# Cross-attention and feed-forward layer on one core: GpSimd's 1024-column subtractions issued as four of 256 columns, its 768-column operations as three

## The chip, the cores and the metric

The kernel runs on one core of a Trainium2 chip. The metric is the device time of one execution in microseconds (us), lower is better. The engines of the core are TensorE (PE in the rows), VectorE (DVE), ScalarE (ACT), GpSimd (POOL) and SyncE (SP), which only issues transfers here. Each engine takes its instructions in the order in which the program gives them and waits at semaphores.

## The reference, cut to what matters

The input is x (2 x 512 rows of 1024 columns, float32), positions and a context of 1024 rows. One layer is computed:

```python
x = x + xattn(layernorm(x), ...)      # 256 channels of 4; 16 heads of 16
x = x + ffn(layernorm(x), ...)

# in xattn, twice (after attention, after the product with the context):
return (hs * A_full + out * B_full).reshape(b, l, H * C)      # rat_write, the residual write

# in ffn, for each of w1, w2, w3 (3584 x 1024 and its transpose):
d = w - base
coeff = mean(abs(d))
W = base + coeff * sign(d)
```

Everything is float32. In the residual write three of the four channels of a row (768 columns) are multiplied by A and have a term q subtracted or added; the fourth (256 columns) only gets a term added. `coeff` needs the mean over a whole weight, so each weight is read twice: once to measure it, once to use it.

## The kernel before

**Two phases.** Phase one (0 to about 450 us of the span) does the whole of the attention layer and, beside it, measures w1 and w3: 56 tiles of 128x1024, each loaded with its base, subtracted, and summed in absolute value on ScalarE. Every third tile is subtracted by GpSimd (`MEASURER = ("DVE", "DVE", "POOL")`), the others by VectorE. Phase two (about 450 us to the end) is the feed-forward layer. Up to about 1000 us it makes the weights w1 and w3 tile by tile and multiplies with them (lines L1501 on TensorE, written as sums and differences of blocks, seven products p1 to p7 for each pair of tiles, in three passes each); after that it multiplies with w2 (L1542) and GpSimd has nothing to do.

**Order.** The order of phase one comes from a list scheduler in the kernel file, `phase_one_order()`. Its table of times holds one of 2.35 us for a subtraction on GpSimd, and it keeps apart in time what it takes for a stretch in which VectorE and GpSimd can't both work (`shared`, `begin`). Phase two's order comes from a second planner, `ffn_order()`. Both give each engine a fixed list; the kernel walks the lists.

**GpSimd's work.** Beside powers of one to three columns (L2459) and the DMAs of w2 (L2520) it has:

- `measure(t)` (L2463): the subtraction of a tile that is measured, 18 times in phase one;
- `difference(n)` (L2468): the subtraction of weight tile n before ScalarE takes its sign, 56 times, 4 of them in phase one. ScalarE's `sign` (L1805; in phase one L1800) waits for it, VectorE's `whole_weight` (L2179) waits for the sign and makes base + coeff * sign; from that come the sums of tiles (L2191 to L2199) and the low parts for the three passes (`lower`, L2183), whose high parts ScalarE writes (L1814, L1822, L1949, L1954);
- part 9 of `rat_out`: the three channels of a residual write, `hid - q` (L2445) for the first write, `q + x` (L2450) for the second, 768 columns, 8 times each;
- part 10 of `rat_out` (L2455): the fourth channel, 256 columns, and L2505 the same columns plus x.

Part 11 on VectorE (L2157, L2160) ends a residual write. In phase two the four row buffers of w1 and w3 are loaded by SyncE (L1179, L1180) as soon as VectorE's last readers of a buffer are done:

```python
if f == 0:
    sp.wait_ge(d_lo, j - 1)
    sp.wait_ge(e_lo, j - 1)
    sp.wait_ge(f_sum, 4 * (j - 1))
```

`d_lo`, `e_lo`, `f_lo`, `g_lo` count the low parts (L2183) of the tiles. ScalarE also copies each product's bank out of PSUM before TensorE may write it again (`snap`: L1959, L1964, L1968); L1968 is the copy after p5, and p3 writes the same bank. VectorE's L2377 to L2390 are the sums of the hidden rows, half tiles of 512 columns from SBUF. TensorE in phase one also has products with a constant (L1344, `pair<-unit`) that no result needs; their number is fixed.

Of the kernel before, what the change touches and what calls it, by code (L numbers as in the profile page):

```python
# [11 lines left out]
ALU = mybir.AluOpType  # L12
# [4 lines left out]
BATCH, SEQ, HID = 2, 512, 1024  # L17
H, C, RH = 256, 4, 16
# [46 lines left out]

UNITS = 3 * JT
PARTS = 3
NB = HID // P
VW = HD + 1
VT = NH * VW + 32 - VW  # L70
# [139 lines left out]
def before(stage, t, part):  # L210
# [105 lines left out]
    elif stage == "measure":  # L316
        if part == 0:
            after("measure", t - PARTS, 2)
            if t >= LATER:
# [490 lines left out]
def bass_layer(nc: bass.Bass, d: dict, out: bass.AP):  # L810
    with ExitStack() as whole:
# [38 lines left out]
        wqkv = sba("wqkv", [P, HH, 3 * H])  # L850
        diag = [sba("diag0", [P, NB, WAYS[0], 32])]
        yn = sba("yn", [P, 3, H])
# [6 lines left out]

        xT = sba("xT", [P, NB, P])  # L860

# [26 lines left out]
        qk_xa = sba("qk_xa", [P, HID])  # L888
# [57 lines left out]
        def measured(t):  # L946

            if t % PARTS == 0:
                return part[:, 0, :], part[:, 1, :]
            n = t % PARTS - 1  # L950
            if t < LATER:
# [6 lines left out]
        ld_x = [sem(f"ld_x{t}") for t in range(TILES)]  # L958
        ld_part = [sem(f"ld_part{n}") for n in range(PARTS)]
        ld_raw = [sem(f"ld_raw{n}") for n in range(ROWS)]  # L960
# [19 lines left out]
        bk_v, fi_v, fi_q, fi_x, fi_var, fi_pow, fi_ok = sems("bk_v fi_v fi_q fi_x fi_var fi_pow fi_ok")  # L980
        me_dve, me_pool, me_abs, c_ones, c_sum, c_mm, c_ok = sems("me_dve me_pool me_abs c_ones c_sum c_mm c_ok")
        n_wk, n_t, n_hi, n_lo, eye_ok = sems("n_wk n_t n_hi n_lo eye_ok")
        f_diff, f_sign, f_w, f_sum = sems("f_diff f_sign f_w f_sum")
# [191 lines left out]
        def _(sp):  # L1175
# [23 lines left out]
            for engine, stage, t, part in order:  # L1199
                if engine != "SP":  # L1200
                    continue
                if stage == "measure":
                    n, j = divmod(t, JT)
                    if t >= PARTS:
                        sp.wait_ge(me_abs, t - PARTS + 1)
                    if t == LATER:
# [125 lines left out]
        def _(pe):  # L1332
# [5 lines left out]
            def turn_hid(t, target):  # L1338

                return turn_blocks(lambda k: hid[:, t, k * P:(k + 1) * P], NB, target)  # L1340

# [1096 lines left out]
        def _(pool):  # L2438
            def rat_out(n, stage, t, part):
                q, skip = (wr[set_of[stage, t]][k] for k in ("q", "s"))  # L2440
                ha, last = by_channel(t)[:, 0:3, :, :], by_channel(t)[:, 3, :, :]
                if part == 9:
                    pool.wait_ge(ro_q[n], t + 1)
                    if n == 0:
                        pool.tensor_tensor(ha, ha, q[:, :].rearrange("p (c k j) -> p c k j", c=C - 1, j=32), ALU.subtract  # L2445
                                           ).then_inc(bk_v, 1)
                    else:
                        pool.wait_ge(fi_v, t + 1)
                        pool.wait_ge(ld_again, again_turn(t))
                        pool.tensor_tensor(q[:, :], q[:, :], qk_xa[:, 0:3 * H], ALU.add).then_inc(fi_q, 1)  # L2450
                elif part == 10:
                    pool.wait_ge(ro_s[n], t + 1)
                    if n == 1:
                        pool.wait_ge(fi_x, t + 1)
                    pool.tensor_tensor(last, last, skip[:, :].rearrange("p (k j) -> p k j", j=32), ALU.add).then_inc(ro_skip[n], 1)  # L2455

            def factors(r, done):

                pool.tensor_tensor(r, r, power[:, 0:r.shape[1]], ALU.pow).then_inc(done, 1)  # L2459

            def measure(t):
                w, base = measured(t)
                pool.tensor_tensor(w, w, base, ALU.subtract).then_inc(me_pool, 1)  # L2463

            def difference(n):
                w, base = raws[n % ROWS]
                pool.wait_ge(ld_raw[n % ROWS], 32 * (n // ROWS + 1))
                pool.tensor_tensor(w[:, :], w[:, :], base[:, :], ALU.subtract).then_inc(f_diff, 1)  # L2468

            pool.memset(power[:, :], -0.5).then_inc(consts, 1)  # L2470
            pool.wait_ge(consts, 1)
# [125 lines left out]
```

## Time and profile before

| | |
|---|---|
| time, three runs | 1272.66 us median (1272.12 to 1275.04) |
| the profiled execution | 1270.68 us, span 1268.9 us, granted TensorE clock 0.989 |
| TensorE busy | 1185.2 us, 93% of the span |
| VectorE busy | 981.4 us, 77% |
| ScalarE busy | 694.1 us, 55% |
| GpSimd busy | 283.4 us, 22%, in 187 instructions |

A row of a timeline has start, duration and then engine, line, operation, tiles and shape; in brackets stands how long the engine had been idle and what ended that. "x2" is two instructions merged, with their common duration. An instruction that has started but can't get on shows it as a longer duration.

### The profile page before, as it was taken

How to read it: one execution, taken by the hardware profiler on the slowest of the kernel's cores; microseconds unless marked ns; L12 is line 12 of the kernel's file. 1: busy time of each engine (PE TensorE's matmuls, PEld its weight loads, DVE VectorE, ACT ScalarE, POOL GpSimd, SP SyncE). 2: the span in 40 equal slices, each digit the busy share in tenths (PEclk: the TensorE clock that was granted, in tenths of full speed). 3: DMA queues.
4: the chain of work that ended last, by engine and by line, in shares of the span. 5: the costliest groups of instructions: out<-in, count | busy, mean ns of one | idle time of the engine just before them, and what ended most of it. 6: DMA issues, size and time to landing. Idle time of an engine off the chain costs nothing. (4 is left out here: it accounts for less than half of the span.)

```text
span 1268.9 us, 17072 instructions
## 1 busy us (share of the span) xinstructions
PE 1185.2 (93%) x6298; PEld 921.5 (73%) x6298; DVE 981.4 (77%) x1287; ACT 694.1 (55%) x999; POOL 283.4 (22%) x187
## 2 busy tenths in 40 slices
PE   5889878898899599999999999999999999999998
PEld 3755455565666478888878888887788888888887
DVE  6878678867787957988887778797786777888864
ACT  4768566574455547565566655565564334334342
POOL 2223223323331212334133333232340000000000
PEclk9999999999999699999999999999999999999999
DMA  9266667865011145768667778766795877853232
GB/s 358 91 243 248 253 242 264 309 245 188 13 67 67 50 149 143 227 220 277 215 216 224 230 240 265 208 203 192 234 287 165 316 279 255 283 198 122 95 126 107
DMA packets 99062, 257.35 MB, mean 203 GB/s; under 512 B 9362, under 2 KB 23972, under 8 KB 98468
## 3 DMA queue, kind: packets, MB, share of 16 engines
q1 hardware_dynamic: 94948, 241.59, 52.7%
q0 software_dynamic: 4032, 14.68, 6.4%
q8 instruction: 50, 0.82, 0.3%
q14 instruction: 32, 0.26, 0.1%
HBM read 214.81 MB, written 41.42 MB: 202 GB/s over the span
## 5 line engine op out<-in xcount | busy, mean ns | idle before, releaser
L2004 ACT ACTIVATE split<-grid 128x1024 fp32r<-128x1024 f32 x98 | 104.0, 1061 | 160.8 <-PE pair L1542 147.4
L2468 POOL TENSOR_TENSOR raw_w<-raw_w,raw_base 128x1024 f32<-128x1024 f32 x56 | 143.5, 2579 | 214.7 <-DMA raw_base<-in_mean_w 214.2
L2412 DVE TENSOR_TENSOR split<-grid,split 128x1024 fp32r<-128x1024 f32 x98 | 119.6, 1224 | 61.9 <-ACT split L2004 61.7
L1542 PE MATMUL quad<-split 128*128 128x512 f32 x588 | 149.3, 389 | 0.5 <-DVE hid L2419 0.5
L1542 PE MATMUL pair<-split 128*128 128x512 f32 x588 | 149.2, 389 | 0.0
L1542 PEld LDWEIGHTS quad<-split 128*128 128x128 f32 x588 | 110.3, 188 | 23.7 <-DVE split L2412 0.9
L1542 PEld LDWEIGHTS pair<-split 128*128 128x128 f32 x588 | 110.4, 188 | 22.9
L1501 PE MATMUL pair<-xnT_hi,ring_hi 128*128 128x512 f32 x224 | 88.1, 393 | 9.6 <-DVE t_b_lo L2215 9.6
L1501 PE MATMUL pair<-t_b_hi,ring_hi 128*128 128x512 f32 x224 | 88.9, 397 | 4.4 <-ACT snap L1968 4.1
L2183 DVE TENSOR_TENSOR ring_lo<-raw_base,ring_hi 128x1024 fp32r<-128x1024 f32 x56 | 68.3, 1220 | 26.4 <-ACT ring_hi L1949 21.0
L1501 PE MATMUL pair<-xnT_hi,ring_lo 128*128 128x512 f32 x224 | 87.9, 392 | 0.0
L1501 PE MATMUL pair<-t_b_lo,ring_hi 128*128 128x512 f32 x224 | 87.9, 392 | 0.0
L1501 PE MATMUL pair<-xnT_lo,ring_hi 128*128 128x512 f32 x224 | 87.8, 392 | 0.0
L1501 PE MATMUL pair<-t_b_hi,ring_lo 128*128 128x512 f32 x224 | 87.2, 389 | 0.0
L2179 DVE SCALAR_TENSOR_TENSOR raw_w<-quad,coeff,raw_base 128x1024 f32<-128x1024 f32 x52 | 66.5, 1278 | 15.1 <-ACT quad L1805 14.8
L2183 DVE TENSOR_TENSOR ring_lo<-raw_w,ring_hi 128x1024 fp32r<-128x1024 f32 x28 | 40.6, 1454 | 41.1 <-ACT ring_hi L1814 41.1
L1805 ACT ACTIVATE quad<-raw_w 128x1024 f32<-128x1024 f32 x52 | 53.0, 1019 | 20.4 <-POOL raw_w L2468 20.1
L2520 POOL DMA_DIRECT2D late<-in_w x28 | 25.0, 892 | 150.9 <-ACT late L1980 150.9
L1501 PEld LDWEIGHTS pair<-xnT_hi,ring_hi 128*128 128x128 f32 x224 | 42.6, 190 | 18.8 <-issue 9.8
L2091 DVE TENSOR_REDUCE negwide<-quad 128x4 f32<-128x512 f32 (+3 forms) x32 | 46.9, 1486 | 11.9 <-PE quad L1438 11.9
L1501 PEld LDWEIGHTS pair<-t_b_hi,ring_hi 128*128 128x128 f32 x224 | 42.1, 188 | 15.4 <-ACT snap L1968 7.0
L2463 POOL TENSOR_TENSOR ctxw<-ctxw 128x1024 f32<-128x1024 f32 x14 | 34.0, 2428 | 80.2 <-DMA ctxw<-in_mean_w 80.2
(332 smaller groups left out, 2784.8 us busy)
## 6 DMA issues: line engine op xcount, KB each, us to landing
raw_w<-in_w SPq DMA_DIRECT2D x56, 512.0 KB, 5.4
raw_base<-in_mean_w SPq DMA_DIRECT2D x56, 512.0 KB, 6.7
grid<-h_blocks SPq DMA_DIRECT2D x49, 512.0 KB, 3.7
ctxw<-in_w SPq DMA_DIRECT2D x28, 512.0 KB, 4.0
ctxw<-in_mean_w SPq DMA_DIRECT2D x28, 512.0 KB, 5.2
late<-in_mean_w SPq DMA_DIRECT2D x28, 512.0 KB, 7.5
late<-in_w POOLq DMA_DIRECT2D x28, 512.0 KB, 6.2
grid<-in_mean_w SPq DMA_DIRECT2D x28, 512.0 KB, 4.7
```

The costliest lines, as they stand in the source:

```text
L1501: a = pe.matmul(bank, ww[:, at + k, :], xx, start=first and k == 0 and n == 0, stop=k == half - 1 and n == 2, skip_group_check=not first)
L1542: a = pe.matmul(into[t], found[:, a, t * P:(t + 1) * P], found[:, b, :], start=p == 0 and n == 0 and q < 4, stop=p == PAIRS - 1 and n == 2 ...
L1805: act.activation(spare.rearrange("p a b -> p (a b)"), w[:, :], ACT.Sign).then_inc(f_sign, 1)
L2004: act.activation(splits[n % RINGS][:, 0:2, :], operands(n), ACT.Copy).then_inc(a_hi, 1)
L2091: a = dve.tensor_reduce(found.rearrange("p r j -> p (r j)"), quad[:, :, at:at + cols], AX.X, ALU.max, negate=True)
L2179: dve.scalar_tensor_tensor(w[:, :], sign, coeff[:, k:k + 1], base[:, :], ALU.mult, ALU.add).then_inc(f_w, 1)
L2183: dve.tensor_tensor(whole_of(pair[1]), source, whole_of(pair[0]).bitcast(F32), ALU.subtract).then_inc(done, 1)
L2412: dve.tensor_tensor(found[:, 2:4, :], operands(n), found[:, 0:2, :].bitcast(F32), ALU.subtract).then_inc(a_lo, 1)
L2463: pool.tensor_tensor(w, w, base, ALU.subtract).then_inc(me_pool, 1)
L2468: pool.tensor_tensor(w[:, :], w[:, :], base[:, :], ALU.subtract).then_inc(f_diff, 1)
L2520: pool.dma_start(lates[n % LATES][:, :], d["w2"][n], accum_op=ALU.add).then_inc(ld_add[n % LATES], 16)
```

## The change

GpSimd's `measure` and `difference` issue four subtractions of 256 columns in place of one of 1024. The two forms of part 9 issue three operations of 256 columns, one for each channel, in place of one of 768. Only the last instruction of a group adds to the semaphore. The planners' tables and all other engines' lists stay as they are.

```diff
+QUARTERS = 4
...
                     if n == 0:
-                        pool.tensor_tensor(ha, ha, q[:, :].rearrange("p (c k j) -> p c k j", c=C - 1, j=32), ALU.subtract
-                                           ).then_inc(bk_v, 1)
+                        for c in range(C - 1):
+                            a = pool.tensor_tensor(ha[:, c], ha[:, c], q[:, c * H:(c + 1) * H].rearrange("p (k j) -> p k j", j=32),
+                                                   ALU.subtract)
+                        a.then_inc(bk_v, 1)
                     else:
                         pool.wait_ge(fi_v, t + 1)
                         pool.wait_ge(ld_again, again_turn(t))
-                        pool.tensor_tensor(q[:, :], q[:, :], qk_xa[:, 0:3 * H], ALU.add).then_inc(fi_q, 1)
+                        for c in range(C - 1):
+                            some = slice(c * H, (c + 1) * H)
+                            a = pool.tensor_tensor(q[:, some], q[:, some], qk_xa[:, some], ALU.add)
+                        a.then_inc(fi_q, 1)
...
+            def subtract(w, base):
+
+                for n in range(QUARTERS):
+                    some = slice(n * HID // QUARTERS, (n + 1) * HID // QUARTERS)
+                    a = pool.tensor_tensor(w[:, some], w[:, some], base[:, some], ALU.subtract)
+                return a
+
             def measure(t):
                 w, base = measured(t)
-                pool.tensor_tensor(w, w, base, ALU.subtract).then_inc(me_pool, 1)
+                subtract(w, base).then_inc(me_pool, 1)
 
             def difference(n):
                 w, base = raws[n % ROWS]
                 pool.wait_ge(ld_raw[n % ROWS], 32 * (n // ROWS + 1))
-                pool.tensor_tensor(w[:, :], w[:, :], base[:, :], ALU.subtract).then_inc(f_diff, 1)
+                subtract(w, base).then_inc(f_diff, 1)
```

GpSimd's list at about 310 to 332 us, before the change: the residual writes of two tiles (`hid` and `wr_q` are the rows and q) and the first four differences (`raw_w`).

```order
66 L2445 TENSOR_TENSOR hid<-hid,wr_q 128x3x8x32
67 L2455 TENSOR_TENSOR hid<-hid,wr_s 128x8x32
68 L2468 TENSOR_TENSOR raw_w<-raw_w,raw_base 128x1024 x2
69 L2459 TENSOR_TENSOR stat_back<-stat_back,power 128x2
70 L2468 TENSOR_TENSOR raw_w<-raw_w,raw_base 128x1024
```

The same place after the change (the line numbers have moved):

```order
66 L2447 TENSOR_TENSOR hid<-hid,wr_q 128x8x32 x3
67 L2461 TENSOR_TENSOR hid<-hid,wr_s 128x8x32
68 L2471 TENSOR_TENSOR raw_w<-raw_w,raw_base 128x256 x8
69 L2465 TENSOR_TENSOR stat_back<-stat_back,power 128x2
70 L2471 TENSOR_TENSOR raw_w<-raw_w,raw_base 128x256 x4
```

Nothing has changed places; the tile of 768 columns is three instructions, each tile of 1024 is four.

GpSimd's list at the end of phase one and the start of phase two (from about 415 us) before the change, with the last two second residual writes, L2450 and L2455:

```order
91 L2450 TENSOR_TENSOR wr_q<-wr_q,qk_xa 128x768
92 L2455 TENSOR_TENSOR hid<-hid,wr_s 128x8x32
93 L2505 TENSOR_TENSOR hid<-hid,qk_xa 128x8x32
94 L2450 TENSOR_TENSOR wr_q<-wr_q,qk_xa 128x768
95 L2455 TENSOR_TENSOR hid<-hid,wr_s 128x8x32
96 L2459 TENSOR_TENSOR x_stat<-x_stat,power 128x1 x2
97 L2468 TENSOR_TENSOR raw_w<-raw_w,raw_base 128x1024
98 L2520 DMA late<-in_w 128x1024
99 L2468 TENSOR_TENSOR raw_w<-raw_w,raw_base 128x1024 x3
```

And after it:

```order
91 L2455 TENSOR_TENSOR wr_q<-wr_q,qk_xa 128x256 x3
92 L2461 TENSOR_TENSOR hid<-hid,wr_s 128x8x32
93 L2518 TENSOR_TENSOR hid<-hid,qk_xa 128x8x32
94 L2455 TENSOR_TENSOR wr_q<-wr_q,qk_xa 128x256 x3
95 L2461 TENSOR_TENSOR hid<-hid,wr_s 128x8x32
96 L2465 TENSOR_TENSOR x_stat<-x_stat,power 128x1 x2
97 L2471 TENSOR_TENSOR raw_w<-raw_w,raw_base 128x256 x4
98 L2533 DMA late<-in_w 128x1024
99 L2471 TENSOR_TENSOR raw_w<-raw_w,raw_base 128x256 x12
```

Again nothing has moved past anything else; between the pieces of one tile stands no other instruction of GpSimd. The lists of TensorE, VectorE, ScalarE and SyncE are the same but for line numbers.

## Rows read from the trace of the kernel before

**Rows 1.** Windows: us, busy time (instructions) per engine, PEclk, DMA share, GB/s

```profile
core 0: us, PE busy (x) PEld busy (x) DVE busy (x) ACT busy (x) POOL busy (x), PEclk, DMA share, GB/s
0.00:450.00 450.00, 374.51 (x2738) 256.98 (x2739) 350.18 (x627) 269.24 (x478) 125.09 (x107) 0.97 0.50 186
450.00:1000.00 550.00, 545.62 (x2395) 445.65 (x2394) 431.54 (x478) 321.51 (x421) 158.32 (x80) 1.00 0.69 221
```

**Rows 2.** Waits of TensorE: who, for whom, us in total, times, longest

```profile
PE pair L1501 <- DVE t_b_lo L2215: 9.6, 1, 9.6
...
PE pair L1501 <- ACT snap L1968: 4.1, 3, 2.1
```

**Rows 3.** Timeline of GpSimd, operations back to back

```profile
196.95 0.72 POOL L2459 TENSOR_TENSOR stat_back<-stat_back,power 128x2 f32<-128x2 f32 x1
197.63 0.73 POOL L2505 TENSOR_TENSOR hid<-hid,qk_xa 128x256 f32<-128x256 f32 x1
...
322.28 4.68 POOL L2468 TENSOR_TENSOR raw_w<-raw_w,raw_base 128x1024 f32<-128x1024 f32 x2
```

**Rows 4.** Timeline, 709 to 716 us, GpSimd and VectorE

```profile
709.27 6.07 POOL L2468 TENSOR_TENSOR raw_w<-raw_w,raw_base 128x1024 f32<-128x1024 f32 x2
...
710.77 2.30 DVE L2183 TENSOR_TENSOR ring_lo<-raw_w,ring_hi 128x1024 fp32r<-128x1024 f32 x1 [2.10 <-ACT ring_hi L1814]
```

**Rows 5.** Groups of VectorE, 450 to 985 us: busy us, mean ns | idle before

```profile
L2191 DVE TENSOR_TENSOR raw_base<-raw_w 128x512 f32<-128x512 f32 x27 | 30.0, 1110 | 0.0
...
L2381 DVE TENSOR_TENSOR work<-work 128x512 f32<-128x512 f32 x13 | 24.1, 1850 | 1.3
...
L2347 DVE TENSOR_TENSOR work<-quad,snap 128x512 f32<-128x512 f32 x26 | 17.8, 684 | 5.8 <-ACT snap L1968 5.8
```

**Rows 6.** Timeline, collisions in phase one, VectorE and TensorE

```profile
44.80 2.29 DVE L2032 SCALAR_TENSOR_TENSOR stat_front<-stat_front 128x3 f32<-128x3 f32 x1 [0.97 <-POOL stat_front L2459]
...
324.87 2.90 DVE L2157 TENSOR_TENSOR hid<-hid,wr_a 128x768 f32<-128x768 f32 x1
...
328.82 1.09 PE L1335 MATMUL pair<-ident,hid 128*128 128x128 f32 x8 [1.13 <-DVE hid L2160]
...
332.00 2.30 DVE L2032 SCALAR_TENSOR_TENSOR stat_back<-stat_back 128x2 f32<-128x2 f32 x1 [0.82 <-POOL stat_back L2459]
...
337.55 0.27 PE L1486 MATMUL pair<-ident,wr_b 128*8 128x128 f32 x1 [1.71 <-DVE wr_b L2131]
...
378.78 1.70 DVE L2028 SCALAR_TENSOR_TENSOR x_stat<-x_stat 128x1 f32<-128x1 f32 x1
...
380.73 0.27 PE L1486 MATMUL pair<-ident,wr_b 128*8 128x128 f32 x1 [1.02 <-DVE wr_b L2131]
```

**Rows 7.** Timeline, the end of phase one, 425 to 439 us

```profile
425.91 1.83 POOL L2450 TENSOR_TENSOR wr_q<-wr_q,qk_xa 128x768 f32<-128x768 f32 x1 [4.33 <-issue]
427.70 1.70 POOL L2455 TENSOR_TENSOR hid<-hid,wr_s 128x256 f32<-128x256 f32 x1
...
426.03 4.46 DVE L2183 TENSOR_TENSOR ring_lo<-raw_w,ring_hi 128x1024 fp32r<-128x1024 f32 x2
...
431.60 0.94 DVE L2157 TENSOR_TENSOR hid<-hid,wr_a 128x768 f32<-128x768 f32 x1
...
438.45 0.76 PE L1501 MATMUL pair<-xnT_hi,ring_hi 128*128 128x512 f32 x1 [9.58 <-DVE t_b_lo L2215]
```

**Rows 8.** Timeline, one round of phase two, 850 to 871 us

```profile
850.91 2.39 POOL L2468 TENSOR_TENSOR raw_w<-raw_w,raw_base 128x1024 f32<-128x1024 f32 x1 [9.67 <-DMA raw_base<-in_mean_w]
850.92 2.93 DVE L2385 TENSOR_TENSOR s_rows<-s_rows,work 128x512 f32<-128x512 f32 x1
...
855.15 1.21 DVE L2183 TENSOR_TENSOR ring_lo<-raw_base,ring_hi 128x1024 fp32r<-128x1024 f32 x1
...
856.39 0.33 SPq L1179 DMA_DIRECT2D raw_w<-in_w  x1
...
866.10 2.39 POOL L2468 TENSOR_TENSOR raw_w<-raw_w,raw_base 128x1024 f32<-128x1024 f32 x1 [9.53 <-DMA raw_base<-in_mean_w]
...
870.16 0.50 PE L1501 MATMUL pair<-t_b_hi,ring_hi 128*128 128x512 f32 x1 [2.06 <-ACT snap L1968]
```

## Prediction

> **What bounds the kernel now.** I began with the busy times by window. From 450 to 1000 us TensorE is busy 545.6 of 550 us at full clock; before 450 us it is busy 374.5 of 450 [rows 1]. So phase two can give back about 4 us up to the point where GpSimd stops, and phase one is where time lies. Its chain passes again and again through VectorE, ScalarE and short products. The waits of TensorE then say what ends last: 9.6 us at the end of phase one on VectorE's L2215, and in phase two three waits, 4.1 us together, on ScalarE's copy L1968 [rows 2]. GpSimd is busy about a quarter of the time in both stretches, so its own length is not the question; what it does to VectorE is. One view shows that: in phase two a half-tile operation of VectorE takes 0.68 us when one input is in PSUM (L2347) but 1.11 us on average in L2191 and 1.85 us in L2381, whose inputs are both in SBUF [rows 5].
>
> **What the two do to each other.** At 710.77 VectorE starts a low part while GpSimd is in a difference that began at 709.27. It takes 2.30 us and not the 1.21 us of a free one [rows 4, 8]: it gets on at about 711.85. The second difference had been queued; the two together end at 715.34. 715.34 less 2.34 is 713.0, and VectorE's operation ends at 713.07: GpSimd, too, waited for VectorE. So one of them works at a time, for a whole instruction, and who has waited comes next, even between two queued instructions of GpSimd. The end of phase one shows it in a row of four: L2450 until 427.7, a low part, L2455 (1.70 us instead of 0.72), the second low part, 4.46 us for a pair that needs 2.35 [rows 7]. The Trainium skill, "SBUF — State Buffer", section "Who interferes with whom", states the same as a rule: a VectorE instruction with two SBUF inputs and a GpSimd instruction that reads SBUF exclude each other, and the later one blocks fully until the other ends. The trace agrees to 0.1 us. By that rule pieces cut both ways: each piece of GpSimd may have to wait for an instruction of VectorE.
>
> **The price of a piece.** GpSimd operations of 256 columns follow each other at 0.68 us (196.95 to 197.63), two of 1024 take 4.68 us, 2.34 each; the one of 768 columns gives way to the next after 1.79 us [rows 3, 7]. (2.34 - 0.68) / 768 is 2.16 ns a column, which leaves 0.13 us fixed for an instruction. Alone, a difference becomes 4 x 0.68 = 2.72 us, 0.38 us more; a residual write 2.04, 0.27 us more. The Trainium skill, "GPSIMD Engine Reference", section 3.1, gives 4497 ns for 2048 columns and about 2.6 cycles a column at 1.2 GHz, 2.17 ns; as an estimate that leaves 0.06 us fixed and 0.18 us more for a difference. The slope agrees with the rows; the fixed part doesn't, and mine stands.
>
> **Phase one.** For each collision I let pieces of 0.68 us and VectorE's next operations take turns, and cap the gain by the idle time of TensorE behind it.
> - 44.80: the three-column L2032 sits behind a whole subtraction, 2.29 us instead of 0.15. Behind a piece it loses 0.6. ScalarE's next step starts 1.6 us earlier; I count 1.0.
> - 324.87 and 332.00: L2157 takes 2.90 instead of 0.95, L2032 2.30 instead of 0.15, and TensorE idles 1.13 and 1.71 us behind them [rows 6]. A third one, at 314.45, is of the same kind on the same chain. By turns they gain 1.3 (314.45), 0.9 (324.87) and, since L2032, L2157 and L2160 then each meet a piece, only 0.2 (332.00): 2.4 in sum.
> - 378.78: the one-column L2028 takes 1.70; with a piece 0.6. TensorE idles 1.02 behind it [rows 6]: 1.0. Two like it, at 230.81 and 388.87, I put at 0.7 and 0.55.
> - The end. From 425.91: piece to 426.59, low part to 427.73, piece to 428.41, low part to 429.55, piece to 430.23, L2179 to 431.43, L2455 to 432.1, L2157 then. It starts at 431.60 now [rows 7]. VectorE there has only operations from SBUF, so each piece takes a turn: four turns of 0.68 in place of 2.1 us. Loss 0.45, and nothing hides it, for this is the wait of 9.58 us.
>
> 1.0 + 2.4 + 1.0 + 1.25 - 0.45 = 5.2 us. Not all arrives: between these places other chains of phase one are nearly as long, and the constant products of TensorE keep their number. From both sides: nothing passes but the loss (+0.45), or all (-5.2). I take 0.6 of it, nearer to all since the caps are already idle time that TensorE shows: **-3.1 us**.
>
> **Phase two.** Take the round at 850 us [rows 8]. Now the difference lies over L2385 (2.93 us), VectorE goes on, its low part ends at 856.36, SyncE issues the next load at 856.39, that lands, the next difference starts at 866.10, and TensorE has idled 2.06 us at 870.16, as the copy L1968 stands behind the sign of that difference in ScalarE's list. By turns: piece to 851.59, L2385 to 852.2, piece to 852.9, L2390 to 853.5, piece to 854.2 beside L2341 (PSUM, no collision), low part to 855.3. The load is issued 1.0 us earlier. The difference at 866.10 has VectorE idle beside it and takes 0.38 longer. The wait of 2.06 becomes about 1.4. The three waits of 4.1 us follow this pattern: 3 x 0.6 = 1.9 us. Against it: the first difference itself ends at 856.0 instead of 853.3, so ScalarE's sign, everything behind it, and VectorE's L2179 (which wants that sign) come 0.9 to 2.7 us later, and the third load of the round about 1.3 us later. What is late then are copies that TensorE wants two products later (2.7 us each), but I know no row that prices the third load. Bounds: -1.9 with no price for it, and +1.1 (3 x 0.38) with the loads no earlier, up to +4 if each of the three waits also gets that 1.3. I take **-1.0 us**. After 1000 us GpSimd does nothing and nothing changes.
>
> **Sum.** -3.1 - 1.0 = -4.1 us. The profiled execution took 1270.7 us (span 1268.9 and 1.8 around it), so its counterpart would be 1266.6. It lies 2.0 below the median of the runs, 1272.66; against that I get **1268.6 us**. A measurement of this kernel tells about 0.2% from no change, 2.5 us.
>
> **Rivals.**
> - *The gain stays local.* VectorE gets its turns sooner, but other chains of phase one end the stages, and phase two breaks even. For it: VectorE's total loss changes little where it has only SBUF work, four turns of 0.68 against one of 2.34. Against: the idle times right behind the collisions. Gain 0 to 2.5, time about 1271.5. Chance 0.26.
> - *Slower: long differences hold ScalarE's list.* In about nine of the 14 rounds the difference at the place of 850.91 grows from 2.4 to over 5 us. If the later sign delays the round's loads, the waits on L1968 grow by 0.38 + 1.3 each instead of shrinking, and rounds that now have no wait get one of about 1 us. It decides when more than three rounds do so, as then phase two costs over 5 us: about 1276. For it: such ScalarE lateness goes to a wait beyond one product, 2.7 us. Against: the first load goes out earlier. Chance 0.12.
> - *GpSimd keeps its turn between pieces.* Pieces overlap a little (0.72 us long, 0.68 apart [rows 3]); if VectorE can't get in between, a tile blocks it for 2.72 us. Each of some nine collisions on the chain costs 0.27 to 0.38 more: +3 us, 1275.5. Against: [rows 4, 7], where it got in between two queued ones. Chance 0.05.
> - *More than I count*: all of phase one's 5.2 and all of 4.1, or a chain freed that I don't see: below 1264. Chance 0.04.
>
> The forecast has 0.53, its own range is 1265 to 1270. The forecast's range reaches from its lower edge over the first rival to the border of the slower ones: 1264.6 to 1273.5. Faster by over 0.2% (below 1270.1): forecast, the last rival and a little of the first, 0.58. Slower (above 1275.2): most of the second and third, 0.15. The rest 0.27.
>
> **What the profile of the changed kernel would show.** Pieces 0.68 us apart where VectorE is idle. VectorE's L2032 at about 45 and 330 us at no more than 0.8 us; L2381 and L2191 at means near 1.0; GpSimd's busy time up by 20 us or more, most of it from waiting. A difference over the half-tile sums of over 4 us. The waits of TensorE on L1968 under 3 us in sum. The 9.58 us before L1501 about unchanged, its start some 3 us earlier. The prediction is wrong if TensorE's start there has not moved (the gain was local), or if the L1968 waits have grown or come in more than three rounds (the long differences).

## Result and the profile after

The changed kernel takes 1259.13 us (median of four, 1257.10 to 1264.21) against 1273.85 of before in the same comparison: ratio 0.9888, 95% interval [0.9853, 0.9923], 14.3 us less (9.8 to 18.7). A second comparison of the same kernel, the run `again` below, gave 1260.38 and 0.9894 [0.9871, 0.9918], 13.5 us. Two executions of later comparisons, one of before with 2399 us and one of eighths_drained with 4158 us, are left out of all ratios. I had forecast 1268.6 within 1264.6 to 1273.5: the direction was right, the gain three and a half times too small, and the time is outside the range.

The page after, first the busy times, then the chain of work that ended last:

```profile
PE 1188.3 (94%) x6298; PEld 925.6 (74%) x6298; DVE 952.1 (76%) x1287; ACT 696.0 (55%) x999; POOL 355.1 (28%) x441
...
PE 86%; DVE 7%; ACT 5%; issue 2%; POOL 0%; DMA 0%; SPq 0%; DVEq 0%; ACTq 0%
```

GpSimd is 71.7 us busier, VectorE 29.3 us less. The windows of after, to be set beside [rows 1]:

```profile
0.00:450.00 450.00, 383.77 (x2762) 265.04 (x2763) 341.20 (x630) 273.14 (x482) 146.25 (x205) 0.95 0.51 186
450.00:1000.00 550.00, 549.58 (x2415) 449.97 (x2414) 418.36 (x482) 324.12 (x422) 208.82 (x236) 1.00 0.72 228
```

TensorE is busy 9.3 us longer in the first 450 us, at a mean granted clock of 0.95 instead of 0.97, and has 24 more products behind it. In the 550 us after that it stands still for 0.4 us where it stood 4.4. Its waits, first of before (those that [rows 2] doesn't have), then of after:

```profile
PE pair L1418 <- DVE negwide L2091: 7.1, 11, 1.6
...
PE quad L1445 <- DVE negwide L2091: 4.0, 3, 2.7
PE pair L1486 <- DVE wr_b L2131: 3.9, 5, 1.7
```

```profile
PE pair L1502 <- DVE t_b_lo L2216: 9.2, 1, 9.2
...
PE pair L1419 <- DVE negwide L2092: 4.2, 9, 0.8
...
PE quad L1446 <- DVE negwide L2092: 3.3, 2, 3.0
...
PE pair L1487 <- DVE wr_b L2132: 1.3, 3, 0.5
...
PE pair L1502 <- ACT snap L1969: 0.4, 1, 0.4
```

VectorE's groups in phase two, 450 to 985 us, beside [rows 5]: the sums from SBUF fall to means of 0.74 and 0.89 us, the form with an input in PSUM is unchanged.

```profile
L2192 DVE TENSOR_TENSOR raw_base<-raw_w 128x512 f32<-128x512 f32 x27 | 20.0, 740 | 0.0
...
L2348 DVE TENSOR_TENSOR work<-quad,snap 128x512 f32<-128x512 f32 x28 | 19.2, 685 | 9.4 <-ACT snap L1969 9.2
...
L2382 DVE TENSOR_TENSOR work<-work 128x512 f32<-128x512 f32 x13 | 11.5, 887 | 1.3
```

**Where the time went, place by place.** TensorE has the same 6298 products in the same order in both traces, so the delay of a product, its start in after less its start in before, says what has been won so far. These are the products of after that answer to 337.55, 380.73 and 438.45 us [rows 6, 7], and one ahead of them that is at 286.52 in before:

```profile
286.91 0.24 PE L1609 MATMUL pair<-csum,ones 128*128 128x2 f32 x1 [0.42 <-issue]
...
334.39 0.27 PE L1487 MATMUL pair<-ident,wr_b 128*8 128x128 f32 x1
...
376.02 0.27 PE L1487 MATMUL pair<-ident,wr_b 128*8 128x128 f32 x1
...
433.10 0.76 PE L1502 MATMUL pair<-xnT_hi,ring_hi 128*128 128x512 f32 x1 [9.25 <-DVE t_b_lo L2216]
```

The delay is +0.39, then -3.16, -4.71 and -5.35 us: 3.55 us between 287 and 335, 1.55 up to 376, 0.64 up to the end of phase one. The two waits for `wr_b` are gone. No fall of the granted clock lies between 287 and 406 us in either trace, so the first two steps are not the clock's. The rest, to -10.1 us at the end, comes at three products of phase two that waited for L1968 in before: 638, 870 and 910 us.

Before 287 us this pair of traces shows no gain on balance, and that is most likely chance. TensorE is 2.3 us ahead at 53 us; then the granted clock takes it back. It falls from 2.4 to 1.2 GHz at other places in each trace: the mean over the first 290 us is 0.99 in before and 0.96 in after. The deepest fall of after, 0.55 in 220 to 230 us, is not the work of the pieces: hold_adds below, which has none, shows 0.51 there. Nor is the one in 50 to 60 us (0.83): first_four, whole up to 314 us, shows 0.73.

The three profiled kernels that leave phase one as it was (before, p2_pieces, hold_adds below) begin phase two at 438.45, 444.12 and 444.43 us; the four with all its pieces (after, again, p1_pieces, p1_and_hold) at 433.10, 431.35, 435.01 and 433.78. The means are 9.0 us apart. The profiled run of before, at a mean clock of 0.989, was among the luckiest: 22 later runs had 0.981 to 0.989 and a median of 1275.1 us, 4.5 above it.

### The profile page after: what moved, and what is told of

Same layout as the page of the kernel before. It is cut to its first block, busy times and chain, and to the rows that moved or that the text cites. A ratio compares the mean times of both kernels' runs of the same rounds, so it can differ in the third digit from the quotient of the medians.

```text
span 1258.8 us, 17326 instructions
## 1 busy us (share of the span) xinstructions
PE 1188.3 (94%) x6298; PEld 925.6 (74%) x6298; DVE 952.1 (76%) x1287; ACT 696.0 (55%) x999; POOL 355.1 (28%) x441
## 4 chain that ended last, share of the span: by engine, by line
PE 86%; DVE 7%; ACT 5%; issue 2%; POOL 0%; DMA 0%; SPq 0%; DVEq 0%; ACTq 0%
PE pair L1502 30%; PE quad L1502 12%; PE quad L1543 10%; PE pair L1543 10%; PE pair L1483 3%; PE quad L1446 2%; PE pair L1599 2%; PE quad L1436 2%; DVE negwide L2092 2%; PE quad L1483 1%; PE quad L1599 1%; ACT prob L1747 1%; PE pair L1409 1%; PE pair L1336 1%; PE pair L1389 1%
## 5 line engine op out<-in xcount | busy, mean ns | idle before, releaser
L2471 POOL TENSOR_TENSOR raw_w<-raw_w,raw_base 128x256 f32<-128x256 f32 x224 | 199.3, 950 | 184.7 <-DMA raw_base<-in_mean_w 184.7
L2184 DVE TENSOR_TENSOR ring_lo<-raw_base,ring_hi 128x1024 fp32r<-128x1024 f32 x56 | 71.4, 1275 | 32.5 <-ACT ring_hi L1950 25.7
L2471 POOL TENSOR_TENSOR ctxw<-ctxw 128x256 f32<-128x256 f32 x56 | 42.5, 790 | 75.4 <-DMA ctxw<-in_mean_w 75.4
L2092 DVE TENSOR_REDUCE negwide<-quad 128x4 f32<-128x512 f32 (+3 forms) x32 | 46.9, 1487 | 13.5 <-PE quad L1439 13.5
L1747 ACT ACTIVATE prob<-quad 128x1536 f32<-128x1536 f32 (+1 forms) x24 | 38.2, 1592 | 23.6 <-PE quad L1451 13.6
```

The lines of the kernel that those rows point to most:

```text
L1747: act.activation(probs[TURN[u] % 2][:, :, 0:cols], quad[:, :, 0:cols], ACT.Exp).then_inc(at_p, 1)
L2092: a = dve.tensor_reduce(found.rearrange("p r j -> p (r j)"), quad[:, :, at:at + cols], AX.X, ALU.max, negate=True)
L2184: dve.tensor_tensor(whole_of(pair[1]), source, whole_of(pair[0]).bitcast(F32), ALU.subtract).then_inc(done, 1)
L2471: a = pool.tensor_tensor(w[:, some], w[:, some], base[:, some], ALU.subtract)
```

## The experiments

Each is timed against before in one of four comparisons, in which before had medians of 1273.5 to 1275.9 us; so the ratios can be set side by side, the medians only roughly. "Idle" is what TensorE stood still between 15 us and its first product of phase two, without the last wait, the one of 9.1 to 10.3 us right ahead of that product. "p5 waits" are those on the copy L1968 (L1969 or L1970 in the changed kernels). Idle, start and p5 waits come from one trace of each kernel.

| kernel | median, us | ratio, 95% interval | idle, us | phase two begins | p5 waits, us |
|---|---|---|---|---|---|
| before (profiled run) | | | 52.0 | 438.5 | 4.1 |
| again (= changed) | 1260.38 | 0.9894 [0.9871, 0.9918] | 44.3 | 431.4 | none |
| p1_pieces | 1263.25 | 0.9910 [0.9890, 0.9931] | 45.8 | 435.0 | 1.9 |
| p2_pieces | 1272.02 | 0.9985 [0.9966, 1.0004] | 54.5 | 444.1 | 0.4 |
| hold_adds | 1271.19 | 0.9977 [0.9957, 0.9997] | 51.7 | 444.4 | none |
| p1_and_hold | 1261.55 | 0.9877 [0.9859, 0.9895] | 42.5 | 433.8 | 0.3 |
| first_four | 1269.61 | 0.9954 [0.9934, 0.9974] | 51.6 | 443.5 | 3.1 |
| measure_only | 1272.66 | 0.9974 [0.9955, 0.9993] | 49.3 | 442.9 | 1.9 |
| writes_only | 1269.47 | 0.9947 [0.9925, 0.9969] | 47.7 | 437.9 | 2.5 |
| halves | 1263.88 | 0.9898 [0.9880, 0.9916] | 45.3 | 438.1 | 1.0 |
| eighths | 1273.10 | 0.9984 [0.9960, 1.0008] | 46.9 | 434.9 | 7.7 |
| eighths_drained | 1267.82 | 0.9942 [0.9920, 0.9964] | 46.3 | 439.7 | 3.3 |
| eighths_add_moved | 1273.98 | 0.9996 [0.9975, 1.0016] | 48.0 | 434.7 | 2.0 |
| quarters_drained | 1260.47 | 0.9890 [0.9860, 0.9919] | 43.6 | 435.5 | none |

**One phase at a time.** In p1_pieces and p2_pieces `subtract` gets the number of pieces:

```diff
-                subtract(w, base).then_inc(f_diff, 1)
+                subtract(w, base, QUARTERS if n < ROWS else 1).then_inc(f_diff, 1)   # p1_pieces
+                subtract(w, base, 1 if n < ROWS else QUARTERS).then_inc(f_diff, 1)   # p2_pieces, measure and part 9 whole
```

Expected of p1_pieces:

> Pieces in phase one alone (measure, both forms of part 9, the four differences of phase one); the 52 differences of phase two are whole again. If the gain of the two phases adds up, as the delay between the two traces says (5.3 us at the first product of phase two, 4.7 us more until 913 us), TensorE's first product of phase two starts near 433 us, the three waits on the copy behind p5 are back at about 4.1 us, and the time is 8 to 10 us below before (5.3 and what the profiled run of the changed kernel lost to a low granted clock before 250 us). If the gain of phase one needs the pieces of phase two, or is given back there, it is under 4 us.

Expected of p2_pieces:

> Pieces in the 52 differences of phase two alone; all of phase one as before. If the gains add up: the first product of phase two starts near 438.4 us as before, the waits on the copy behind p5 are under 0.6 us in sum, and the time is 4.7 us below before, 4 to 5.5. My recorded step (each wait shrinks by 0.6, less the price of long differences) gives 1 us.

Measured: 11.5 us (8.8 to 14.0) for phase one alone, above the 8 to 10 expected, though the interval reaches into it; 1.9 us (-0.5 to 4.3) for phase two alone, where 4 to 5.5 was expected, and by its interval not clear of zero. They add up to the 13.5 of the whole. Phase one is over four fifths of the gain. The waits on the copy are back in p1_pieces at 1.9 us, not 4.1. In p2_pieces the delay against before falls from +5.7 to +0.9 us during phase two, so 4.8 us against that trace; but p1_pieces, with phase two whole, falls by 1.8 too. The three waits of the profiled run of before, 4.1 us, add up to more than those of the other traces with whole differences in phase two (1.9 to 3.1). TensorE's whole idle time between its first product of phase two and the end of the work on w1 and w3 is 2.2 to 4.4 us in these five traces and 0.0 to 0.6 in the five with quarters.

Expected of again:

> The changed kernel once more, for a second trace. If the profiled run lost its early gain to the granted clock by chance, the delay against before at 50 us (2.3 us less) stays in part until 450 us when the clock is 0.989 or more, and the first product of phase two starts 7 to 8 us earlier than 438.45 instead of 5.3. If the clock falls because of what the change does to TensorE before 250 us, it falls at the same places again (0.55 in 220 to 230 us) and the start is at 433 us again.

Its products are 2.2 us ahead at 53 us, level with before at 219 us, and 7.1 ahead at 431 us; the clock falls at the same places as in the first trace of this kernel (50, 140, 180 and 220 us), in 220 to 230 us to 0.71, not 0.55. The second expectation held for the places, not for the size, and the start is 7.1 us ahead as the first one had it. Neither decides whether the falls are the change's; hold_adds does, which has the fall at 220 to 230 us without any pieces.

**Which pieces of phase one.** Each of three kernels cuts one kind of tile:

```diff
+                subtract(w, base, QUARTERS if n < ROWS else 1).then_inc(f_diff, 1)   # first_four, all else whole
+                subtract(w, base).then_inc(me_pool, 1)                               # measure_only, all else whole
+                        for c in range(C - 1):                                       # writes_only: part 9, all else whole
```

Expected of first_four:

> Only the first four differences of weight tiles (314, 322, 324 and 332 us in the profile of before) are four pieces each; measuring tiles, residual writes and the 52 differences of phase two are whole. My recorded step for this place is 2.4 us, of which 0.6 arrives: 1.4 us. The delay between the two traces says 3.5 us at the first product behind it (337.55), all of it kept until 438 us: 3.5 us faster, 2.5 to 4.5.

Expected of measure_only:

> Only the 18 measured tiles are in quarters. Recorded step: 1.0 us at 44.80, x 0.6. From the traces of the changed kernel: TensorE 2.2 us earlier at 53 us, 0.6 to 1.7 of it kept at 60 us. If the phase-one gain of 11 us (that kernel with phase one's pieces alone) is 3.5 at the first four differences and 2.2 at the second residual writes, some 5 us are left, and measuring is the larger part of them: 3 to 5 us. If measuring is a local matter, under 1.5 us.

Expected of writes_only:

> Only part 9 of the residual writes is in three pieces. Recorded step: 1.0 at 378.78, 0.7 at 230.81, 0.55 at 388.87, less 0.45 at the end, x 0.6 = 1.1 us. The delay between the traces says 1.6 at 380.73, 0.3 at 397 and 0.3 at 415 to 438, nothing that can be seen apart at 230: 2.2 to 3 us faster.

Measured: 5.9 us (3.3 to 8.4), 3.3 (0.9 to 5.7) and 6.8 (4.0 to 9.6). measure_only is inside its expectation. first_four is above its 2.5 to 4.5, though its interval reaches into it, and the stretch between the traces is the 3.5 us expected (1.3 up to 328, 2.3 more up to 337). The writes are worth two to three times what I saw at single places. The sum of 16 is above the 11.5 of all three together. The intervals allow that, and there is a reason for part of it: the wait at 328.82 shrinks from 1.13 to 0.28 us in writes_only and to nothing in first_four, and the one at 236.26 (1.59) is gone in measure_only and in writes_only, so each is counted twice. writes_only removes 1.5 us between 345 and 381 us, and measure_only 1.5 between 30 and 53 us.

**The order of two loads.** In hold_adds all operations are whole, as in before. GpSimd only issues four of the w2 loads (L2520) later, when SyncE may issue the weight tile that the next difference needs:

```diff
+HELD = (37, 41, 45, 49)
...
                 elif task == "wadd":
                     pool.wait_ge(w_neg, n + 1)
+                    coming = [m for what, m in mine[place:] if what == "diff"][:1]
+                    if coming and coming[0] in HELD:
+                        pool.wait_ge(f_lo, coming[0] // 2 - 1)
+                        pool.wait_ge(g_lo, coming[0] // 2 - 1)
```

> The kernel before with whole operations; GpSimd issues the accumulating load of w2 in four rounds (before differences 37, 41, 45, 49) only when SyncE may issue the load of that weight tile. Theory A, the order of issue in the DMA queues: in these rounds the tile's load then goes out level with or ahead of the w2 load and lands in 5 to 7 us after issue in place of 6.8 to 9.6; the waits of TensorE at 870 and 910 us (2.06 and 0.97) shrink to under 0.5 each, that at 638 (1.15, its round isn't touched) stays; 2 to 3 us faster than before. Theory B, what counted was that the low part got its turn sooner and so the load was issued 1.0 to 1.4 us sooner: nothing changes, 4.1 us of waits, time as before.

Theory A holds. The round of [rows 8] had this issue of the w2 load 0.71 us ahead of SyncE's at 856.39:

```profile
855.68 0.89 POOL L2520 DMA_DIRECT2D late<-in_w  x1 [2.39 <-ACT late L1980]
```

In hold_adds it stands 0.51 us behind:

```profile
860.71 0.33 SPq L1180 DMA_DIRECT2D raw_w<-in_w  x1
...
861.22 0.89 POOL L2524 DMA_DIRECT2D late<-in_w  x1 [3.61 <-issue]
866.59 2.40 POOL L2469 TENSOR_TENSOR raw_w<-raw_w,raw_base 128x1024 f32<-128x1024 f32 x1 [4.48 <-DMA raw_base<-in_mean_w]
```

From the issue to the difference it is 5.88 us instead of 9.71. Over the four rounds the tile lands 7.99, 6.79, 9.63 and 8.72 us after its issue in before, 5.23, 5.35, 5.80 and 5.49 here. All waits on the copy are gone, also the one at 638 us, whose round isn't touched and which I had expected to stay; it is missing in p1_pieces and first_four too, so it belongs to the trace of before and not to the order of the loads. The kernel is 2.9 us faster (0.4 to 5.5), as much as pieces in phase two bring within the intervals. The changed kernel does the same by itself, in the same round:

```profile
848.99 0.33 SPq L1180 DMA_DIRECT2D raw_w<-in_w  x1
...
849.07 0.89 POOL L2533 DMA_DIRECT2D late<-in_w  x1 [2.39 <-ACT late L1981]
...
856.00 0.73 POOL L2471 TENSOR_TENSOR raw_w<-raw_w,raw_base 128x256 f32<-128x256 f32 x1 [6.05 <-DMA raw_base<-in_mean_w]
```

VectorE's low part ends sooner, so SyncE's load is issued 1.4 us earlier (against TensorE's products) and gets level with or ahead of the w2 load; over the four rounds it lands 4.81, 4.95, 6.94 and 5.55 us after its issue.

p1_and_hold puts this edit on p1_pieces.

> Pieces in phase one alone, as before, and the w2 loads of four rounds held behind the weight tile's load; the 52 differences of phase two whole. If phase two's gain in the changed kernel is only the order in which the two loads go out, this kernel equals the changed one: 1259 to 1261 us, waits on the copy behind p5 under 0.5 us. If the shorter turns of phase two bring something of their own, it stays at the time of phase one's pieces alone, 1263.

Its ratio, 0.9877, is that of the changed kernel within the intervals, and 4 us better than that of p1_pieces, though those two intervals touch (0.9895 and 0.9890); the p5 waits are 0.3 us. As far as the runs can tell, the pieces in phase two bring nothing that whole differences with the right order of loads don't have.

**The size of a piece.** `QUARTERS = 2` and `QUARTERS = 8`.

Expected of halves:

> The changed kernel with its 1024-column tiles in two operations of 512 (part 9 stays in three). An instruction of VectorE then waits up to 1.24 us for its turn (2.16 ns a column and 0.13), between 0.68 and 2.34. If the gain goes with the length of one turn, TensorE's idle time in phase one lies between the 44.4 us of quarters and the 52.7 of whole tiles, at 46 to 48, and the time is 2 to 4 us above the changed kernel: 1262 to 1264. If all that counts is that VectorE gets in once, it equals the changed kernel, 1260.

Expected of eighths:

> The changed kernel with its 1024-column tiles in eight operations of 128 columns (part 9 stays in three). If what counts is how long one instruction of VectorE waits for its turn (0.68 us behind a quarter, about 0.41 behind an eighth by 2.16 ns a column and 0.13 fixed), phase one gains a little more, 0.5 to 1.5 us below the changed kernel, 1259. If each piece costs a wait of its own for VectorE where VectorE works without a pause, the differences in phase two grow from 4.3 to 8 us and more, the signs behind them come later, and the waits on the copy behind p5 come back: 1 to 4 us above the changed kernel, 1262 to 1264.

Halves: 1263.88 is the time that the first expectation had, but before was slow in that comparison too (1275.86), and the ratio of 0.9898 is that of quarters (0.9888 and 0.9894). So the times don't tell halves from quarters. At one place the traces do: the wait of 1.71 us at 337.55 is still 1.44 in halves and nothing with quarters or eighths.

Eighths begin phase two as early as quarters, but the time is 11 us above the changed kernel, beyond both expectations. One wait of TensorE of 5.07 us behind this place is the largest part. The granted clock then falls to 0.69 in 720 to 730 us, where the changed kernel has 1.00; with the waits taken off, phase two is 3.0 us longer than in after. The other 2.6 us of p5 waits lie at 519 to 640 us. The rows ahead of the wait of 5.07:

```profile
708.25 0.89 POOL L2533 DMA_DIRECT2D late<-in_w  x1 [6.89 <-ACT late L1981]
708.87 10.19 POOL L2471 TENSOR_TENSOR raw_w<-raw_w,raw_base 128x128 f32<-128x128 f32 x24
...
709.81 10.34 DVE L2184 TENSOR_TENSOR ring_lo<-raw_w,ring_hi 128x1024 fp32r<-128x1024 f32 x1 [1.55 <-ACT ring_hi L1815]
```

24 pieces, 0.42 us apart, and VectorE's low part, 1.2 us when free, gets no turn among them. The changed kernel has it too, with eight pieces, and so has p1_pieces with two whole differences:

```profile
702.17 0.89 POOL L2533 DMA_DIRECT2D late<-in_w  x1 [8.54 <-ACT late L1981]
702.78 5.86 POOL L2471 TENSOR_TENSOR raw_w<-raw_w,raw_base 128x256 f32<-128x256 f32 x8
...
704.05 5.68 DVE L2184 TENSOR_TENSOR ring_lo<-raw_w,ring_hi 128x1024 fp32r<-128x1024 f32 x1 [1.87 <-ACT ring_hi L1815]
```

```profile
704.71 0.89 POOL L2533 DMA_DIRECT2D late<-in_w  x1 [9.93 <-ACT late L1981]
705.33 5.07 POOL L2471 TENSOR_TENSOR raw_w<-raw_w,raw_base 128x1024 f32<-128x1024 f32 x2
...
706.18 5.31 DVE L2184 TENSOR_TENSOR ring_lo<-raw_w,ring_hi 128x1024 fp32r<-128x1024 f32 x1 [1.45 <-ACT ring_hi L1815]
```

In each the run of pieces starts 0.62 us after a transfer's issue began that itself takes 0.89. Two kernels ask whether that is the condition. One lets GpSimd wait for a small operation of its own behind each issue, the other moves the issue behind the first difference:

```diff
                     pool.dma_start(lates[n % LATES][:, :], d["w2"][n], accum_op=ALU.add).then_inc(ld_add[n % LATES], 16)
+                    pool.memset(power[:, :], -0.5).then_inc(drained, 1)
+                    pool.wait_ge(drained, n + 1)
```

```diff
+            place = mine.index(("diff", 29))
+            mine.insert(place + 1, mine.pop(place - 1))
```

Expected of eighths_drained:

> The kernel with eighths, and behind each of GpSimd's w2 loads in phase two a memset of its own (128x3, the constant that is there already) for which GpSimd then waits, so that no piece follows a transfer's issue directly. In the eighths kernel the 24 pieces that start 0.62 us after the issue at 708.25 run for 10.2 us without a gap, VectorE's low part of 1.2 us takes 10.34 beside them, and TensorE then waits 5.07 us. Theory A, pieces that are queued while the issue still runs leave VectorE no turn until the run is over: here that low part takes under 2 us, the waits on the copy behind p5 fall from 7.7 to about 2 us, and the time is 4 to 6 us below the eighths kernel, 1266 to 1269 us. Theory B, GpSimd keeps its turn whenever enough short pieces are queued, whatever stands ahead of them: the low part still takes 8 us or more and the time stays at the eighths kernel's, 1271 to 1273.

Expected of eighths_add_moved:

> The kernel with eighths, and the w2 load at 708.25 issued behind difference 29 and not ahead of it. Theory A, what counts is the issue directly ahead of a run: VectorE's low part meets the eight pieces of difference 29 with nothing ahead of them and takes under 2 us. What is starved then is whatever VectorE has beside differences 30 and 31, which now follow the issue. The w2 load goes out some 4 us later, which its reader on ScalarE may feel, so only the durations are read here, the time not closely. Theory B: the low part still waits for all pieces that are queued, 3 us for one difference and more.

Expected of quarters_drained:

> The changed kernel with the same memset and wait behind each w2 load. Theory A: the 5.7 us low part at 704 us falls to under 2 us; TensorE's waits on the copy behind p5, 0.4 us in the changed kernel, can't give back more, so the time is that of the changed kernel within 1 us, 1259 to 1261. Theory B: neither changes.

Theory A in all three, read by the low parts. With the wait in between, 16 pieces run at the same place and VectorE has its turn among them:

```profile
712.89 0.89 POOL L2533 DMA_DIRECT2D late<-in_w  x1 [6.89 <-ACT late L1981]
713.49 0.41 POOL L2534 MEMSET power<- 128x3 f32 x1
713.98 7.74 POOL L2471 TENSOR_TENSOR raw_w<-raw_w,raw_base 128x128 f32<-128x128 f32 x16
...
714.45 1.49 DVE L2184 TENSOR_TENSOR ring_lo<-raw_w,ring_hi 128x1024 fp32r<-128x1024 f32 x1 [1.55 <-ACT ring_hi L1815]
```

The p5 waits fall from 7.7 to 3.3 us, not to 2, and the ratio from 0.9984 to 0.9942. What is left of them lies at 524 to 645 us, as in eighths. That the kernel is still 6 us behind quarters is explained only in part by them. With the issue moved the low part at 707.79 takes 1.33 us, and the same starvation turns up where another issue now stands directly ahead of a run:

```profile
744.14 0.89 POOL L2535 DMA_DIRECT2D late<-in_w  x1 [2.39 <-ACT late L1981]
744.76 6.90 POOL L2471 TENSOR_TENSOR raw_w<-raw_w,raw_base 128x128 f32<-128x128 f32 x16
...
744.82 7.92 DVE L2184 TENSOR_TENSOR ring_lo<-raw_base,ring_hi 128x1024 fp32r<-128x1024 f32 x1 [0.64 <-ACT ring_hi L1950]
```

Here TensorE waits 4.2 us for this low part itself, which the column of p5 waits doesn't show, and its clock falls to 0.66 in 750 to 760 us.

quarters_drained takes the 5.7 us low part down to 1.24 and gains nothing: TensorE has no wait left there. No kernel here is faster than the changed one beyond the intervals.

**The end of phase one.** last_write_whole is the changed kernel with part 9 of the last tile in one operation (`parts = 1 if t == TILES - 1 else C - 1`), of which there is one execution, the profiled one (1259.8 us).

> The changed kernel with the last of the second residual writes in one operation of 768 columns, for the end of phase one alone. My recorded step says that the three pieces there cost 0.45 us: the stretch from the start of the last wr_s operation on VectorE (426 us in before) to the end of its last hid operation before the statistics takes 7.3 to 7.4 us here against 7.75 with pieces. If pieces cost nothing there, as the stretch of the kernel before says (7.85 us), it takes 7.8 to 7.9.

```profile
418.73 0.41 DVE L2154 TENSOR_TENSOR wr_s<-wr_s,quad 128x256 f32<-128x256 f32 x1
419.06 4.46 DVE L2184 TENSOR_TENSOR ring_lo<-raw_w,ring_hi 128x1024 fp32r<-128x1024 f32 x2
...
425.62 0.96 DVE L2161 TENSOR_TENSOR hid<-hid,wr_q 128x768 f32<-128x768 f32 x1
```

The stretch is 7.85 us long, as in before; the changed kernel, with pieces, needs 7.75. The 0.1 us is no scatter: to the end of the last residual write the stretch takes 11.37 to 11.40 us in the ten traces with pieces there and 11.47 to 11.49 in the six without. These are the rows of the changed kernel:

```profile
420.76 3.37 DVE L2184 TENSOR_TENSOR ring_lo<-raw_w,ring_hi 128x1024 fp32r<-128x1024 f32 x2
424.06 1.74 DVE L2180 SCALAR_TENSOR_TENSOR raw_w<-raw_w,coeff,raw_base 128x1024 f32<-128x1024 f32 x1
425.73 1.47 DVE L2158 TENSOR_TENSOR hid<-hid,wr_a 128x768 f32<-128x768 f32 x1
...
420.65 4.07 POOL L2455 TENSOR_TENSOR wr_q<-wr_q,qk_xa 128x256 f32<-128x256 f32 x3 [3.65 <-issue]
424.68 1.70 POOL L2461 TENSOR_TENSOR hid<-hid,wr_s 128x256 f32<-128x256 f32 x1
```

## Why the prediction was right in kind and wrong in size

- **Turns by whole instructions.** Right in phase one. The collisions of [rows 6] at 44.80, 324.87 and 332.00 are these in the trace of after, 0.67, 1.29 and 0.68 us instead of 2.29, 2.90 and 2.30:

```profile
44.06 0.67 DVE L2033 SCALAR_TENSOR_TENSOR stat_front<-stat_front 128x3 f32<-128x3 f32 x1 [0.97 <-POOL stat_front L2465]
...
323.88 1.29 DVE L2158 TENSOR_TENSOR hid<-hid,wr_a 128x768 f32<-128x768 f32 x1
...
329.81 0.68 DVE L2033 SCALAR_TENSOR_TENSOR stat_back<-stat_back 128x2 f32<-128x2 f32 x1 [0.81 <-POOL stat_back L2465]
```

  The three pieces at the end of phase one alternate with VectorE as I had written it down. Of GpSimd's extra 71.7 us, where I had said 20 or more, some 32 are the pieces' own cost by the 0.38 and 0.27 us of the prediction, and the rest is waiting for such turns: the 224 pieces of the differences have a mean of 0.95 us instead of some 0.7.
- **"Not all arrives", the factor 0.6.** This step failed. TensorE has the same products in the same order in all sixteen traces. So each place can be read by itself, by the delay over a stretch without a fall of the clock or by the wait that is gone (times as in before):

| place | counted, us | kept at 0.6 | measured |
|---|---|---|---|
| 44.80 | 1.0 | 0.6 | 1.5, delay between 30 and 53 us |
| 230.81 | 0.7 | 0.4 | 1.4, the wait at 236.26 |
| 314.45 to 332.00 | 2.4 | 1.4 | 3.55, delay between 287 and 338 |
| 378.78 | 1.0 | 0.6 | 1.1, and 0.5 just ahead of it that I had not counted |
| 388.87 | 0.55 | 0.3 | 0.3 to 0.5 |
| the end | -0.45 | -0.3 | +0.1 |

  The sum is 5.2 us as counted, 3.1 as kept and some 8.5 as measured. The starts of phase two are 9.0 us apart, and TensorE's idle time ahead of them is 52.7 us on average without pieces (before, p2_pieces, hold_adds) and 43.9 with (after, again, p1_pieces, p1_and_hold), 8.8 less. So next to nothing is lost on the way, and the factor, for which I had no row, took off 2.1 us. That other chains of phase one would take over is refuted: the waits at 328.82, 337.55 and 380.73 (1.13, 1.71 and 1.02) are gone in every kernel with all pieces of phase one, and still stand in p2_pieces and hold_adds (1.10 or 1.13, 1.71, 1.02).
- **The caps and the turns were too small as well.** Even the full 5.2 us is 3.8 short of the 9.0. The largest item is the group at 314 to 332: I let L2032, L2157 and L2160 meet a piece each and kept 0.2 of the wait of 1.71 at 337.55, and the whole of it went. At 44.80 I counted 1.0 of the 1.6 that I saw, and 1.5 came. At 230.81 I had half the price, since I looked for a wait of TensorE directly behind; it comes 5 us later, behind VectorE's unbroken list. These are two rows of before; the first operation takes 0.18 us in after (232.55):

```profile
230.81 1.22 DVE L2141 TENSOR_SCALAR wr_r<-wr_z 128x48 f32<-128x48 f32 x1
...
236.26 0.44 PE L1418 MATMUL pair<-ident,negwide 128*128 128x128 f32 x2 [1.59 <-DVE negwide L2091]
```

  This wait is 1.59, 1.65, 0.87 and 1.53 us in before, p2_pieces, hold_adds and first_four and nothing in the other twelve traces. It is the clearest of the waits for `negwide`, which are 10.7 to 12.4 us in the three kernels with phase one whole and 6.6 to 9.3 in the four named above. The rest of that difference isn't separated: the wait at 188.42, for one, is 1.34 us in before and in p1_pieces and nothing in hold_adds, so it comes and goes without the change.
- **The 0.45 us at the end.** Wrong in sign but small: 0.1 us gained. My row of turns started the L2157 of 431.60 0.5 us late; against TensorE's products it started 0.6 us early and lost 0.5 in a turn of its own. The working didn't agree with itself either: four turns of 0.68 in place of 2.1 us are 0.62 more, not 0.45.
- **Phase two, -1.0.** The direction was probably right, and the timed runs put the size at 1.9 us (-0.5 to 4.3); but the step was wrong. I let the load be issued 1.0 us earlier and land 1.0 earlier. It is issued 1.4 earlier and lands up to 3 us sooner after its issue, since it no longer stands behind GpSimd's w2 load. hold_adds and p1_and_hold show that this order alone is enough for the gain. The upper bound of +4 was a slip too: 1.1 and three times 1.3 are 5.0. Nothing hangs on it.
- **The base.** I took the profiled run as 2.0 us below the median of three; against later medians it is 3.2 (1273.85) to 4.5 below (1275.1, 22 runs). That made the forecast 1 to 2 us too low and so hid that much of the error in the gain.
- **Rivals.** "The gain stays local" is refuted: the start of phase two moved by 9.0 us on average. "Long differences hold ScalarE's list": the differences over the half-tile sums did grow past 4 us (4.31 at 842.37), yet the waits on L1968 fell. "GpSimd keeps its turn" is refuted as a rule for pieces (0.67 us at 44.06 is one turn), but true in one place, which I had read the other way: at 709.27 [rows 4] I took the second difference for queued. Its tile landed at 711.78, so GpSimd stood still and VectorE got in. In p1_pieces, where the second tile is there, VectorE waits for both.

## What to carry to other kernels

In this kernel a short VectorE operation on the chain lost up to one whole GpSimd instruction each time the two met in SBUF (2.29 us behind 1024 columns, 0.67 behind 256). Pieces of 256 columns cost 0.13 us each and took 8.8 us of waits from TensorE; pieces of 128 took no more. To price such a change, count the waits of the bounding engine behind each collision in full until a row says otherwise, and follow the blocked engine's list for some us, not only to the next instruction. A load that comes late may need nothing but another transfer issued half a microsecond later.

## What the runs showed that I had not expected

- GpSimd instructions that start 0.62 us behind the start of its own transfer issue (0.89 us) shut VectorE out for the whole run of queued ones: 5.3, 5.7, 7.9 and 10.3 us in the rows above. Two runs that start later behind the issue don't: 0.69 us behind it in halves (673.69) and 0.74 in eighths (931.46) VectorE gets in after the first piece. The pieces of such a run show 1.0 us each at 0.70 apart, those elsewhere 0.73 at 0.68 to 0.70. That the next one is then always ready when one ends is my reading of it, not shown; that a wait behind the issue ends it is shown.
- Two 512 KB loads issued 0.04 to 0.71 us apart by different engines: being behind GpSimd's w2 load instead of 0.51 us ahead of it costs the tile 1.4 to 3.8 us (before against hold_adds); the smallest cost goes with the 0.04.
- Between runs of one kernel the granted clock, 0.981 to 0.989 on average, goes with some 0.8 us for each 0.001, by a line through the timed runs of before and of these kernels. As a base the one profiled run was 4.5 us off, more than the 4.1 us of gain that I had forecast.
